# A two-layer attention and expert kernel: stacks of 25 rows, a ring of three one-bank buffers, and row maxima by half batch

## What is computed

```python
Q, K, V = proj(layernorm(x), w_q, b_q), proj(ctx, w_k, b_k), proj(ctx, w_v, b_v)
Q, K = _apply_rope(Q, cos, sin), _apply_rope(K, cos, sin)
scores = jnp.einsum('bhqd,bhkd->bhqk', Q, K) / math.sqrt(DK)
scores = jnp.where(mask == 0, -1000000000.0, scores)
attn = jax.nn.softmax(scores, axis=-1)
ctx = jnp.einsum('bhqk,bhkd->bhqd', attn, V)
x = x + ctx.transpose(0, 2, 1, 3).reshape(b, -1, D) @ w_o.T + b_o
x = x + experts0(layernorm(x))        # 32 routed experts and 8 that pass x on, top 6
x = x + attention1(layernorm(x), ctx) # one head of 128, padding mask
x = x + experts1(x)                   # 8 experts, the nearest centroid's
```

## Time and profile before

| | |
|---|---|
| timed runs | 344.03 us median of 3 (341.42, 344.03, 351.15) |
| the profiled execution | 340.95 us, span 338.6 us |
| mean TensorE clock | 0.94 of 2.4 GHz |
| busy, of the span | PE 87%, DVE 65%, ACT 47%, POOL 46% |
| first score matmul | 27.15 us |
| last score matmuls of pass B | 132.62 us |
| first matmul of the experts | 135.44 us |
| first Silu | 137.61 us |

### The profile page before, as it was taken

One profiled execution on the slowest core, in us unless ns is written; L12 is line 12 of the kernel. 1 busy time (PEld: TensorE's weight loads), 2 busy tenths in 40 slices (PEclk: granted clock), 3 DMA queues, 4 the chain that ended last, 5 costly groups with the idle time before them and its releaser, 6 DMA issues.

```text
span 338.6 us, 4644 instructions
## 1 busy us (share of the span) xinstructions
PE 293.8 (87%) x1570; PEld 189.8 (56%) x1570; DVE 221.0 (65%) x485; ACT 160.2 (47%) x278; POOL 156.1 (46%) x174
## 2 busy tenths in 40 slices
PE   3637899899999898898799969969998996999993
PEld 1422454354445454556577746847765674777771
DVE  4825686565778555786975774497587478666662
ACT  1110034445554576655555527735455844445541
POOL 6365033122212333294686744384655266465551
PEclk9955569999999999999999979997999999899999
DMA  7697936328401020201110100200000000001001
GB/s 211 206 130 206 195 109 185 67 77 149 90 2 51 15 64 2 62 0 20 44 39 27 62 0 0 64 0 0 0 4 0 0 2 0 0 0 33 0 2 31
DMA packets 10247, 18.17 MB, mean 54 GB/s; under 512 B 1328, under 2 KB 7024, under 8 KB 9712
## 3 DMA queue, kind: packets, MB, share of 16 engines
q1 hardware_dynamic: 8496, 11.59, 15.4%
q10 hardware_dynamic: 1728, 6.29, 6.4%
HBM read 15.19 MB, written 2.62 MB: 53 GB/s over the span
## 4 chain that ended last, share of the span: by engine, by line
PE 51%; DVE 16%; DMA 12%; POOL 7%; ACT 5%; issue 4%; SPq 4%; POOLq 0%; ACTq 0%; DVEq 0%
PE psum L1032 47%; DMA qk_scratch<-parts 6%; DMA ctxk<-ctx_tok 3%; DVE early L1002 2%; DVE xn L898 2%; DVE negmax L983 2%; DVE early L1008 2%; DMA pvT<-mask_k 2%; POOL big L546 1%; DMA big<-qk_scratch 1%; ACT early L686 1%; POOL parts L546 1%; DVE stats L727 1%; SPq L383 1%; SPq L368 1%
## 5 line engine op out<-in xcount | busy, mean ns | idle before, releaser
L1002 DVE TENSOR_TENSOR early<-early,psum 128x512 f32<-128x512 f32 x64 | 43.7, 683 | 49.2 <-ACT early L686 49.0
L686 ACT ACTIVATE early<-psum 128x512 f32<-128x512 f32 x64 | 38.3, 598 | 67.4 <-PE psum L1032 67.3
L546 POOL TENSOR_TENSOR parts<-early,parts 128x512 fp32r<-128x512 f32 x32 | 41.3, 1290 | 49.4 <-ACT parts L678 49.4
L1032 PE MATMUL psum<-xs,ws 128*128 128x512 f32 x192 | 56.5, 431 | 0.0
L1032 PE MATMUL psum<-xs,big 128*128 128x512 f32 x192 | 54.9, 422 | 0.0
L983 DVE TENSOR_REDUCE negmax<-psum 128x4 f32<-128x1024 f32 x32 | 39.1, 1222 | 23.3 <-PE psum L1032 23.2
L648 ACT ACTIVATE early<-psum 128x1024 f32<-128x1024 f32 x32 | 32.7, 1023 | 30.9 <-PE psum L1032 30.8
L1008 DVE TENSOR_TENSOR early<-early,psum 128x512 f32<-128x512 f32 x64 | 44.0, 687 | 4.3 <-POOL big L546 1.6
L1032 PE MATMUL psum<-maskb,id 128*128 128x512 bf16 x128 | 43.2, 423 | 2.0 <-DVE negmax L983 1.9
L1032 PEld LDWEIGHTS psum<-big 32*128 32x128 f32 (+1 forms) x256 | 21.0, 203 | 38.7 <-issue 29.8
L1032 PE MATMUL psum<-big 32*128 32x256 f32 (+1 forms) x256 | 35.1, 355 | 7.0 <-DMA big<-qk_scratch 6.9
(11 more groups left out here) (180 smaller groups left out, 436.1 us busy)
## 6 DMA issues: line engine op xcount, KB each, us to landing
raw<-experts ACTq DMA_DIRECT2D x12, 512.0 KB, 3.7
big<-qk_scratch SPq DMA_DIRECT2D x24, 128.0 KB
qk_scratch<-parts SPq DMA_DIRECT2D x16, 128.0 KB, 2.5
big<-qk_scratch SPq DMA_DIRECT2D x16, 64.0 KB
early<-sel SPq DMA_DIRECT2D x2, 512.0 KB, 7.7
ropet<-rope SPq DMA_DIRECT2D x2, 256.0 KB, 4.7
ctxk<-ctx_tok SPq DMA_DIRECT2D x1, 512.0 KB, 9.4
out<-x_in SPq DMA_DIRECT2D x2, 256.0 KB, 3.1
```

The lines of the kernel that those rows point to most:

```text
L546: nc.gpsimd.tensor_tensor(hs(n)[:, 1, :], h32[:, n % 2, :], hs(n)[:, 0, :].bitcast(F32), ALU.subtract).then_inc(lo_ready, 1)
L686: nc.scalar.activation(sg[:, n % 2, :], psum[:, n % 2, :], ACT.Silu).then_inc(silu_ready, 1)
L1002: nc.vector.tensor_tensor(sg[:, n % 2, :], sg[:, n % 2, :], psum[:, 2 + n % 2, :], ALU.mult).then_inc(up_read, 1)
L1032: return nc.tensor.matmul(o, w, r, start=start, stop=stop, skip_group_check=True)
```

## The change

- The stacks get 24 rows per head, [high, high, low] of the queries against [high, low, high] of the keys (low times low is dropped), plus row 25. Four heads lie beside each other at partitions 0, 32, 64 and 96, four deep, and there is room for all four batches. A slot still takes two heads: those at 0 and 32 or those at 64 and 96.
- SP builds them with 2 writes of 256 KB and 16 reads per batch (8 of 16 rows of 4 KB, 8 of 8 rows of 4 KB), and 4 DMAs bring the ones, in place of POOL's memsets.
- Pass A has a ring of three one-bank buffers (banks 0 to 2), and DVE takes the maxima of one head at a time (128x512 in place of 128x1024, two per slot). Pass B has banks 3 and 4, PV bank 5, which ACT copies out after every quad (256 columns).
- maxT is made per half batch, with four transposes in place of two; ACT copies it out and sends it by its own DMA queue. B_START is 7, SLOTS 40.
- On PE a slot is now: A's first mask, small tasks, A's second mask, A's scores, maxT, PV, B's masks, B's scores.
- ACT's order in a slot is: its evictions, the copy to `pvT`, the exponential, other tasks. DVE has tasks first, then the reductions.
- The selectors' staging moves from `early` to `pvT` and `ctxk`, which is loaded later; the csum matmul becomes a task.

```diff
-B_START = PAIRS + LAG
+A_RING = 3
+B_START = 7
@@ slot_tasks
-        if s == PAIRS * (b + 1) - 1:
-            tasks.insert(0, ("maxT", b))
+    if s % (PAIRS // 2) == 0 and s // (PAIRS // 2) <= 2 * B:
+        tasks.append(("maxT", s // (PAIRS // 2) - 1))
@@ banks
+        def a_bank(s, r):
+            return (2 * s + r) % A_RING
+        def b_bank(t, r):
+            return r if t + B_START >= A_SLOTS and (t + B_START - A_SLOTS) % 2 == 1 else A_RING + r
+        def head_rows(i, r, n):
+            g = 2 * (i % 2) + r
+            return slice(32 * g, 32 * g + n)
@@ sync: stack_batch
                 sp.wait_ge(qks_ready, 2 * b + 1)
                 write(1, scratch_k[b])
-                sp.wait_ge(scratch_k[b], 32)
-                read_both(1, 0, 0)
+                sp.wait_ge(scratch_k[b], 16)
+                for g in range(4):
+                    read_both(1, g)
                 sp.wait_ge(qks_ready, 2 * b + 2)
                 write(0, scratch_q[b])
-                read_both(1, 0, 16)
-                read_both(1, 1, 0)
-                read_both(1, 1, 16)
-                sp.wait_ge(scratch_q[b], 32)
-                for r in range(2):
-                    read_both(0, r, 0)
-                    read_turned(r)
+                for g in range(4):
+                    read_one(1, g, 0)
+                sp.wait_ge(scratch_q[b], 16)
+                for g in range(4):
+                    read_twice(0, g)
+                    read_one(0, g, 1)
@@ scalar
+                elif name == "maxT":
+                    if b >= 2:
+                        act.wait_ge(maxrow_in[b - 2], 16)
+                    evict(task, maxrow[:, b % 2, :], m[0:4, :])
+                    act.wait_ge(misc_act, misc_reads(task))
+                    nc.scalar.dma_start(stacks[24:128:32, 0, b // 2, ...], maxrow[:, b % 2, :])
@@ vector, end of a slot
+                    dve.wait_ge(scores_max, s + 1)
+                    for r in range(2):
+                        nc.vector.tensor_reduce(negmax[:, b % 2, :, i // 2, 2 * (i % 2) + r],
+                                                psum[:, a_bank(s, r), :].rearrange("p (t k) -> p t k", t=QT), AX.X,
+                                                ALU.max, negate=True).then_inc(maxes_read, 1)
@@ tensor, a slot
+                def mask_a(r):
+                    if 2 * s + r >= A_RING:
+                        pe.wait_ge(maxes_read, 2 * s + r - A_RING + 1)
+                    mm(psum[:, a_bank(s, r), :], id16[:, :], maskb[:, 0, :, :], True, False)
+                if has_a:
+                    mask_a(0)
+                for task in tasks:
+                    if task[0] != "maxT":
+                        misc_task(*task)
+                if has_a:
+                    mask_a(1)
+                    ...
+                            last_a = scores_a(q, r)
+                    last_a.then_inc(scores_max, 1)
+                ...
+                if t >= 2 and t % 2 == 0:
+                    pe.wait_ge(exps_done, 2 * quad + 2)
+                    if quad >= 1:
+                        pe.wait_ge(pv_evicted, quad)
+                    ...
+                if has_b:
+                    reads = t if t >= 1 and b_bank(t - 1, 0) == b_bank(t, 0) else t - 1
+                    if reads >= 1:
+                        pe.wait_ge(exps_done, reads)
+                    ...
+                            last_b = scores_b(k, r)
+                    last_b.then_inc(scores_exp, 1)
```

229 lines of the change are left out of this document (101 added, 128 removed).

## The result

| | before | after |
|---|---|---|
| timed runs, median | 344.03 us (341.42, 344.03, 344.07; and one of 351.15) | 354.87 us (4 runs, 352.26 to 355.85) |
| the profiled execution, span | 338.6 us | 352.1 us |
| first scores | 27.15 us | 27.77 us |
| clock goes from 1.2 to 2.4 GHz | 48.75 us | 54.01 us |
| last score matmuls of pass B | 132.62 us | 142.98 us |

The changed kernel takes 1.035 times as long (95% interval 1.026 to 1.045, which is 9 to 15 us). The forecast was 347.0 us, range 341 to 353: the direction of the likeliest case was right, its size was not. It takes 10.8 us more by the medians, 13.5 by the spans. Most kernels here have some slower executions, so the medians are of those within 1.5% of the kernel's fastest, and the tables give their number.

The account below looks back on a forecast made before the run. PE was taken to set the stretch to B's last scores, with 5.26 us idle. +3.6 us there and +0.9 to the first Silu made +4.5 on 342.5, so 347.0 us; own range 343 to 351, with rivals 341 to 353.

Parts of the forecast that it names:

- I leave 48.75: PE's clock was forecast to rise from 1.2 to 2.4 GHz at 48.75 us, as before the change.
- behind that nothing is changed: From the first Silu to the end, the time was forecast to stay as before, about 201 us.
- Work to B's last scores: PE's work up to B's last scores, at 2.4 GHz: 90.15 + 2.6 (maxT) + 0.54 (logits) = 93.3 us.
- The start: First scores, waiting for DMA, forecast at 25.5 us in place of 27.15, bounds 22.8 and 31.8.
- Waits where both passes run: Slots 7 to 31: PE waits 1.4 us for the exponential and 1.7 us behind DVE's tasks, 3.1 us in all.
- The B-only slots: Slots 32 to 39: PV in front waits for the exponential, 0.91, 1.13 and 0.69 us, sum 2.7 us.
- To the first Silu: From B's last scores: experts start at +4.15 us, Silu at +5.8 to 5.9 in place of 4.99, so +0.9 us.
- The sign that I had named for being wrong: PE's clock leaving 0.50 (1.2 GHz) at another time than 45 to 52 us would show the forecast wrong.
- 1 (the clock rises earlier): Denser mix from B's earlier start raises PE's clock, from 42 us on saving 3.4 us: 343.6 us; chance 0.12.
- 2 (reads at 52 GB/s): 16-row stack reads also run at 52 GB/s; first scores at 31.8 us, total 351.2 us; chance 0.18.
- 3: Heads at partitions 0 and 32 don't run beside each other on PE: +27 us, 374 us; chance 0.03.
- 4: ACT or DVE fall behind, late by 0.2 us in 25 slots: +5, 352 us; chance 0.10.

Follow-up runs that it names:

- e5: e4 with maxT as two transposes of eight columns in place of four of four; median 347.48 us.
- o4: o2 with maxT as two transposes of eight columns in place of four of four; median 335.54 us (1 of 10 executions).
- e12: e6 with batch 0's four low-part query reads issued from ScalarE's queue, not SyncE's; median 346.41 us.
- e2: Changed kernel with pass A's banks in a ring of five, not three, while A is alone (slots 0 to 5); median 352.89 us.
- e9: e6 with the order within a slot of before the change on PE, DVE and ACT; median 339.50 us (4 of 10 executions).
- e1: Changed kernel with PV behind B's scores, and its copy behind the exponential, in slots 32 to 39; median 349.59 us.
- a1: Changed kernel with only the order within a slot of before restored on three engines, PV's place in the tail included; median 351.63 us.
- o3: o2 with B's masks ahead and both passes' eight score matmuls interleaved over four row groups in 25 slots; median 337.20 us.
- e11: e6 with pass B begun at slot 11 in place of 7; median 348.44 us (2 of 4 executions).
- e6: e4 with PV behind B's scores in all slots, not only 32 to 39; median 345.51 us.
- e3: Changed kernel with pieces 1 to 12 of the experts' weights issued and split one slot earlier; median 349.32 us (1 of 4 executions).
- e4: Changed kernel with the edits of e1, e2 and e3 together; median 346.11 us.
- o2: e9 with batch 0's low-part query reads on ScalarE's queue and x_in of batches 2 and 3 ahead of batch 1's stack; median 336.59 us.

## Why the prediction was wrong

The sum was +4.5 us; by the profiled executions it is +13.5. The step that failed most is the clock: "I leave 48.75" and "behind that nothing is changed" put it at nothing, at its rise and at the experts' start, and it makes some 4.8 of the 9.0 us that were missing. Step by step:

- **Work to B's last scores: right.** I had 93.3 us at 2.4 GHz, of which 2.6 for maxT. With the missing records put back it is 92.8 up to there. And 16 fewer transposes brought 2.1 us in e5 and 1.5 in o4, 0.09 to 0.13 each, where I had 0.11. -0.5.
- **The start: failed.** "25.5 us" came from transfer rates, with 0.35 us for an issue. It was 27.77. The transfers allow 25.06, as e12 shows with the issues on two queues. The term that I left out is issue time: four reads of the keys at 0.69 us each put the queries' write at 15.99 and not 14.84, and the eight query reads take 4.9 us to be issued. At half price, +1.1.
- **"I leave 48.75": failed.** The clock rose at 54.01, which is 5.3 us more at half price: +2.6. Its rise lay between 43 and 77 us in the kernels here, so that to keep it where it was had nothing behind it.
- **The slots of pass A alone: not in the sum.** I looked at the ring of three where both passes run, and not where A is alone. Before it had two pairs of banks there. The mask waits for a reduction in each of these slots; e2 took these waits away. PE idles 1.3 us in the cold stretch: at half price, +0.6.
- **Waits where both passes run: right in kind, a little small.** I had 3.1 us; PE idles 4.2 us in that stretch. Its masks wait for DVE's tasks where I had them, in slots 11, 19 and 27: 0.2, 0.8 and 0.4 us, forecast 0.3, 0.9 and 0.5. The exponential is in it as forecast, in single waits like 0.57 us. What I had not seen are a wait of maxT for the bank that `ctxn` is read from (0.35) and one for `ctxnT` (0.38). +1.1. e9 shows that the order makes most of this and of the next item: idle time falls to 3.2 in all.
- **The B-only slots: right, somewhat small.** Forecast 0.91, 1.13 and 0.69; measured 1.17, 1.12 and 1.01. I had let tasks hide a part that they don't hide, and 1.16 us of maxT's wait stand here too (4.5 us idle against 2.7): +1.8. e1 confirms the mechanism.
- **To the first Silu.** The experts' first matmul came 4.23 us after B's last scores, behind the twelfth piece of weights, as I had it; forecast was 4.15 (its terms add up to 4.10). But Silu came at 7.2 and not 5.8 to 5.9, as the clock fell there: +1.3. Behind Silu it is another +0.9, with the clock still at half for 2.9 us.

These are -0.5 + 1.1 + 2.6 + 0.6 + 1.1 + 1.8 + 1.3 + 0.9 = 8.9 of the 9.0 us. The sign that I had named for being wrong, a clock that leaves 0.50 at another time than 45 to 52, is the one that came.

Rivals: 1 (the clock rises earlier) was wrong here, and right for the interleaved kernels (43 and 44 us). 2 (reads at 52 GB/s) didn't happen: neither a start at 31.8 nor a wait for the stacks of batches 2 and 3, and e12's 25.06 leaves no room for such a rate. The start was late for another reason. But the wait at slot 16 is near: a1 and o3, whose PE comes there earlier, have it with 2.14 and 2.20 us. 3 didn't happen; heads at 0 and 32 run as those at 0 and 64 (0.43 us), even all four. 4 came nearest in its time, 352, but not in its reason: ACT is busy for 37.75 of 72.10 us, and what is late is one exponential whose cover had been moved away.

What stays open is why the clock rises at one time or another: no part of the change is shown to set it, and in e11 nothing in the profile but a longer A-only stretch tells it from e6. The items above are read from one execution of each kernel, and the clock blurs them: e1, e3 and e4 had 3.4 us at half clock between 85 and 92 us as well, which the changed kernel's execution had not.

## What to carry to other kernels

Where an order of work is moved, walk it through each kind of slot apart, also the ones at the beginning and the end where only one pass runs: a rotation of buffers or a place for PV that is free in the middle was paid there. Count what an issue costs its queue when a load becomes many small or broadcast ones, and then look for the load that stands next in that queue. And a stall in front of a dense stretch costs more than its length where the clock falls with it; repairs of such stalls are to be tried together, since one by one they may show little. And before work and idle time are read from a profile, count the matmuls against their weight loads: here the missing records made 2.6 us of work look like none.

## What the runs showed of the hardware

- An issue on SP's queue took 0.44 us for a plain 128-partition write, 0.35 (keys) or 0.46 (queries) for a read of 8 rows, and 0.66 to 0.69 for a read of 16 rows in three dimensions or with a broadcast, and for the one-partition ones (kernel after).
- Eight score matmuls of 24 and 25 rows over four row groups took 0.44 us (o3), the same as four over two.
- A maxT transpose of four or eight columns cost 0.09 (o4 against o2) to 0.13 us (e5 against e4) among other matmuls.
- The granted clock stayed at 1.2 GHz with PE busy 97% of 22.4 us (e11), and fell about the start of the experts in each of the five kernels that had the late piece or the tail's PV waits, and in none of the others. It was also at half in a1 from 75.8 to 79.2 us, behind the wait of 2.14 us, and in o3 from 68.3 to 75.1, about the end of the wait of 2.20.
